# Two-layer GNN in split fp32: the DRAM layout of the adjacency and of x, and the loads that read them

## What is computed

```python
# layer 0
deg = jnp.sum(adj, axis=-1, keepdims=True)
agg = jnp.einsum('bij,bjf->bif', adj, x) / jnp.maximum(deg, EPS)
cat = jnp.concatenate([x, agg], axis=2)
out = relu(jnp.einsum('bnf,of->bno', cat, W))
x = _layernorm(x + out)
# layer 1
Ah = adj + eye
dh = rsqrt(jnp.sum(Ah, axis=-1))
An = dh[:, :, None] * Ah * dh[:, None, :]
out = relu(jnp.einsum('bnm,bmf,fc->bnc', An, x, kernel) + bias)
x = _layernorm(x + out)
```

## Time and profile of the kernel before

| | us |
|---|---|
| median of 3 runs | 506.6 |
| lowest, highest run | 506.44, 506.66 |
| profiled execution, its own time | 506.57 |
| its span in the profile | 504.8 |

### The profile page before, as it was taken

How to read it: one execution, slowest core, us unless ns; L and a number is a source line. 1 busy time by engine, 2 the same in 40 slices (tenths; PEclk the granted TensorE clock), 3 DMA queues, 4 the chain that set the end, 5 groups by cost and what they waited for, 6 DMA issues and landing times.

```text
span 504.8 us, 8135 instructions
## 1 busy us (share of the span) xinstructions
PE 491.4 (97%) x2750; PEld 430.7 (85%) x2750; DVE 393.8 (78%) x960; ACT 327.8 (65%) x601; POOL 0.7 (0%) x6
## 2 busy tenths in 40 slices
PE   7999999999999999999999999999999999999992
PEld 5988788988889888998889988898888988889992
DVE  4786898669966799667996679966898669976656
ACT  5795948757677657766586574955847757576422
POOL 0000000000000000000000000000000000000000
PEclk9999999999999999999999999999999999999997
DMA  7999517944097621955239361593607932061002
GB/s 259 409 373 359 208 48 251 374 120 174 6 349 270 201 90 66 369 188 208 83 117 396 113 211 77 200 385 82 246 1 258 366 115 93 0 208 43 1 0 83
DMA packets 26686, 93.38 MB, mean 185 GB/s; under 512 B 2864, under 2 KB 2992, under 8 KB 26672
## 3 DMA queue, kind: packets, MB, share of 16 engines
q1 hardware_dynamic: 26672, 93.20, 51.1%
HBM read 84.80 MB, written 8.39 MB: 185 GB/s over the span
## 4 chain that ended last, share of the span: by engine, by line
PE 96%; DVE 1%; DMA 1%; ACT 0%; issue 0%; ACTq 0%; SPq 0%
PE ring_b L688 23%; PE ring_b L690 23%; PE ring_b L689 23%; PE ring_a L688 9%; PE ring_a L690 9%; PE ring_a L689 9%; DMA adj_raw<-adjT 1%; DVE stats L521 0%; DVE x L513 0%; DVE u L509 0%; PE ring_b L721 0%; PE ring_b L729 0%; PE ring_b L725 0%; ACT adj_hi L268 0%; ACT x L333 0%
## 5 line engine op out<-in xcount | busy, mean ns | idle before, releaser
L688 PE MATMUL ring_b<-adj_hi,x_hi 128*128 128x512 f32 x254 | 99.4, 391 | 0.0
L689 PE MATMUL ring_b<-adj_lo,x_hi 128*128 128x512 f32 x254 | 99.0, 390 | 0.0
L690 PE MATMUL ring_b<-adj_hi,x_lo 128*128 128x512 f32 x254 | 99.0, 390 | 0.0
L688 PE MATMUL ring_b<-adj_hi,x1s_hi 128*128 128x512 f32 (+1 forms) x256 | 98.3, 384 | 0.0
L690 PE MATMUL ring_b<-adj_hi,x1s_lo 128*128 128x512 f32 (+1 forms) x256 | 98.0, 383 | 0.0
L689 PE MATMUL ring_b<-adj_lo,x1s_hi 128*128 128x512 f32 (+1 forms) x256 | 97.9, 382 | 0.0
L268 ACT ACTIVATE gath_hi<-ring_b 128x512 fp32r<-128x512 f32 (+1 forms) x64 | 36.6, 583 | 64.8 <-PE ring_b L690 64.7
L444 DVE TENSOR_TENSOR adj_lo<-adj_raw,adj_hi 128x1024 fp32r<-128x1024 f32 (+1 forms) x68 | 76.0, 1158 | 3.4 <-ACT adj_hi L268 3.4
L283 ACT ACTIVATE adj_nat<-adj_nat 128x1024 f32<-128x1024 f32 x64 | 67.1, 1052 | 5.0 <-DMA adj_nat<-adjN 4.9
L268 ACT ACTIVATE adj_hi<-adj_raw 128x1024 fp32r<-128x1024 f32 (+1 forms) x68 | 64.9, 999 | 0.8 <-DMA adj_raw<-adjT 0.6
L444 DVE TENSOR_TENSOR gath_lo<-ring_b,gath_hi 128x512 fp32r<-128x512 f32 (+1 forms) x64 | 42.7, 678 | 22.1 <-ACT gath_hi L268 22.1
(11 more groups left out here) (87 smaller groups left out, 940.2 us busy)
## 6 DMA issues: line engine op xcount, KB each, us to landing
adj_nat<-adjN SPq DMA_DIRECT2D x64, 512.0 KB, 5.8
adj_raw<-adjT SPq DMA_DIRECT2D x60, 512.0 KB, 9.7
out<-x SPq DMA_DIRECT2D x15, 512.0 KB, 3.3
xt_raw<-xT SPq DMA_DIRECT2D x7, 1024.0 KB, 4.9
x_sb<-x SPq DMA_DIRECT2D x14, 512.0 KB, 5.1
adj_raw<-adjT SPq DMA_DIRECT2D x8, 256.0 KB, 6.4
x_sb<-x SPq DMA_DIRECT2D x4, 256.0 KB, 6.2
xt_raw<-xT SPq DMA_DIRECT2D x2, 512.0 KB, 12.0
```

Source lines behind the costliest of these rows:

```text
L688: nc.tensor.matmul(o, lhi, rhi, start=(first and i == 0), stop=False)
L689: nc.tensor.matmul(o, lhi, rlo, start=False, stop=False)
L690: last = nc.tensor.matmul(o, llo, rhi, start=False, stop=last_part)
```

## The change

The host lays adjT out as (batch, half, tile, partition, 512), so that one tile of one half is 256 KB without a gap. It lays x out as (batch, pair of tiles, partition, 512), so that one pair is 256 KB without a gap. The destinations in SBUF and everything that the engines compute on stay as they are. The twelve first loads of batch 0 (lines 204 to 206) now each read one piece of 256 KB. A chunk of the adjacency (line 188) and a half of x (line 192) are now two such pieces, with 2 KB for each partition from each, where they were 4 KB for each partition.

```diff
--- before.py
+++ after.py
@@ -186,10 +186,14 @@
             def load_adj(n, h, chunks=range(CH)):
                 for i in chunks:
                     sp.dma_start(raw[:, h, i * JC:(i + 1) * JC, :],
-                                 adjT[n, h, :, i * JC:(i + 1) * JC, :]).then_inc(raw_loaded[h][i], 16)
+                                 adjT[n, h, i * JC:(i + 1) * JC].rearrange("j p m -> p j m")
+                                 ).then_inc(raw_loaded[h][i], 16)
 
             def load_x(n, h):
-                sp.dma_start(x_half(x_sb, h), x_half(x[n], h)).then_inc(x_loaded[h], 16)
+                pairs = CH // H
+                sp.dma_start(x_half(x_sb, h).rearrange("p (i t) c -> p i (t c)", i=pairs),
+                             x[n, pairs * h:pairs * (h + 1)].rearrange("i p m -> p i m")
+                             ).then_inc(x_loaded[h], 16)
 
             def load_rows(n, t):
                 i = t % NR
@@ -201,10 +205,10 @@
 
             for i in range(CH):
                 loaded = x_first_loaded[i // 2] if i % 2 == 0 else x_loaded[i // 2]
-                sp.dma_start(x_pair(x_sb, i), x_pair(x[0], i)).then_inc(loaded, 16)
-                sp.dma_start(raw[:, 0, JC * i, :], adjT[0, 0, :, JC * i, :]).then_inc(raw_first_loaded[i], 16)
+                sp.dma_start(x_pair(x_sb, i).rearrange("p t c -> p (t c)"), x[0, i]).then_inc(loaded, 16)
+                sp.dma_start(raw[:, 0, JC * i, :], adjT[0, 0, JC * i]).then_inc(raw_first_loaded[i], 16)
                 sp.dma_start(raw[:, 0, JC * i + 1, :],
-                             adjT[0, 0, :, JC * i + 1, :]).then_inc(raw_loaded[0][i], 16)
+                             adjT[0, 0, JC * i + 1]).then_inc(raw_loaded[0][i], 16)
             sp.dma_start(w_raw, w).then_inc(w_loaded, 16)
             sp.dma_start(xt_target(0, 1), xt_source(0, 0, 1)).then_inc(xt0_loaded[0], 16)
             load_rows(0, 0)
@@ -862,9 +866,9 @@
 
     x, adj, w, k, bias = (np.asarray(a) for a in (x, adj, L0_gnn_W, L1_gnn_kernel, L1_gnn_bias))
     arrays = {
-        "adjT": adj.reshape(B, H, NH, T, P).transpose(0, 1, 4, 3, 2),
+        "adjT": adj.reshape(B, H, NH, T, P).transpose(0, 1, 3, 4, 2),
         "adjN": adj.reshape(B, T, P, N).transpose(0, 2, 1, 3),
-        "x": x.reshape(B, T, P, F).transpose(0, 2, 1, 3),
+        "x": x.reshape(B, CH, JC, P, F).transpose(0, 1, 3, 2, 4).reshape(B, CH, P, JC * F),
         "xT": x.reshape(B, XP, T // XP, P, FT, P).transpose(0, 1, 5, 2, 4, 3).reshape(B, XP, P, T // XP * FT * P),
         "w": w.reshape(F, 2, FT, P).transpose(3, 2, 1, 0).reshape(P, FT, 2 * F),
         "k": k.reshape(FT, P, F).transpose(1, 0, 2),
```

## The result

The changed kernel takes 504.78 us (median of 6 runs, 504.41 to 505.13) against 506.56 us beside it, a ratio of 0.9963 with a 95% interval of 0.9952 to 0.9973. The forecast was 506.1 with 505.0 as its lower end. In a second comparison on another chip it took 504.63 us, ratio 0.9949 (0.9934 to 0.9964). The gain is 1.8 us in the first comparison and 2.3 in the second.

A forecast was written before the change was run, and what follows sets the result against it. The prediction took TensorE, busy 97% of the span, as the bound, with time to win only in the slow opening loads. It summed -0.6 us (first two loads) and +0.1 (2 KB chunks) to -0.5: 506.1 us, range 505.0 to 507.6.

The forecast's parts named there:

- The bound: Whole kernel: TensorE, busy 97% of the span; time to be had lies between the first adjacency load's issue at 1.18 and 6.23.
- the first two loads: Opening: 0.524 MB of x and adjacency without gaps; first adjacency tile lands 0.6 us sooner, range 0.1 to 0.8.
- the rate of xT's opening: Opening: xT, read without gaps, moved 213 GB/s in its first two microseconds; taken as the new loads' rate, giving 0.6 us.
- a bound from above: Opening: 0.5 MB issued at 107.00 took 4.7 us; two such loads from 0.75 would be down at 5.45, 0.8 us sooner.
- The check of what TensorE needs next: Behind TensorE's start: tile 2 has 1.5 us in hand, the projection 1.2, the fourth degree 0.7; all hold 0.6 us.
- The rival with the clock: TensorE's first products: a shorter gap brings the fast clock forward, about 1.0 on top of 0.6, 505.0 us; chance 0.22.
- The 2 KB chunks: Batch 0's four half 1 chunk loads: 5.6 us at 376 GB/s against 5.1 at 413, 0.5 us more queue.
- The row tiles of adjN: Before the fourth degree: row tile lands at 27.0, wanted at 27.2; just holds, 0.1 us charged for the thin margin.
- There is no slack there: From the fourth degree to TensorE's wait at 61.19: what ScalarE loses at 27.79 is lost to the end.
- The stop at 61.19: TensorE's 0.29 us wait for the gathered low parts, the one stop before the tail; to stay no longer than 0.4.
- The steady batches: Later batches: 1.2 us more loading each, hidden by early landings, costed at nothing; without cover up to 8 us over seven.
- the slower rival: Batch 0's queue: twelve loads without gaps each begin badly, slipping 5.3 us, or half; 508.0 us taken; chance 0.16.

The follow-up runs named there:

- first_only: Kernel before, with only batch 0's twelve first loads (x and adjacency) reading copies without gaps; 504.26 us, ratio 0.9950.
- x_only: Kernel before, with only x laid out anew and the adjacency as before; 504.99 us, ratio 0.9968.
- after_again: The changed kernel, unedited, measured once more beside the kernel before on another chip; 504.63 us, ratio 0.9949.
- x_pitch8448: Kernel before, with batch 0's four loads of x reading a copy with rows 8448 bytes apart; ratio 0.9972.
- x_pitch32k: Kernel before, with batch 0's four loads of x reading a copy with rows 32 KB apart; ratio 0.9976.
- x_pitch10k: Kernel before, with batch 0's four loads of x reading a copy with rows 10 KB apart; ratio 0.9961, one 2812 us execution left out.
- x_pitch8k: Control: kernel before, with batch 0's four loads of x reading a copy with rows still 8 KB apart; ratio 0.9994.

## Why the prediction was wrong

**The bound was read rightly.** The gain was made in the opening: first_only shows it by leaving the rest alone. The part from the first issue to TensorE's start gave 2.1 us; the speed of the first products and the supply of tiles behind them gave and took the rest before 18 us.

**The step that failed is "the first two loads".** It is one term of the sum, 0.6 us, and it measured 2.1. Two readings in it were at fault. I took the rate of xT's opening, 213 GB/s, as that of the new pattern; it was 291. The 213 holds half a microsecond at 49 GB/s, and the new opening has no such hole after its first half microsecond:

```profile
1.75:2.25 0.50, 0.50 (x5) 0.50 (x4) 0.00 (x0) 0.28 (x1) 0.00 (x0) 1.00 0.73 139
2.25:2.75 0.50, 0.50 (x4) 0.50 (x4) 0.00 (x0) 0.00 (x0) 0.00 (x0) 1.00 0.98 336
```

And I took 0.8 us as a bound from above, from x's own later load at 107.00, down after 4.7 us, whose rows are 8 KB apart too: the bound was read off the very pattern that is slow. In the changed kernel the same load, issued at 105.10, is down after 3.7 us. "Strided against without gaps" was the wrong question for x's landing; the runs put that lag on one pitch of six, 8 KB. With x on time the adjacency's 16 KB cost the start 0.2 us (5.00 in x_only, 4.80 in first_only), but its layout still gives part of the time, and no run says by which property. The opening's 146 GB/s was the hint, and the spread of the 16 landings of the first load, which the prediction didn't read, shows seven engines on time and nine not.

**The check of what TensorE needs next left out tile 1.** I named tiles 2 and on. Tile 1's low part was ready at about 8.2 before, 1.5 us ahead of its use at 9.73, and would have been wanted at 7.6 after a gain of 2.1 us. It became the one new wait, 1.10 us in this profile. With 0.6 us this would not have shown; with the true size it decides.

**The rival with the clock had the time, 505.0, and part of the mechanism.** Its sign appeared: the products were fast 1 us after the first, not 3.5. They did speed up sooner, worth 0.87 us in this profile, and in the kernel before the clock alone is worth 1.1. But the changed kernel doesn't live on it: with 8 warming matmuls, and eight slow products, it kept nearly all of its gain. It lives on the loads.

**The 2 KB chunks cost less than I charged.** I charged 0.5 us of queue by the stretch of 376 GB/s, as if the size of the pieces had held it down; with the same 2 KB and no gaps it moves 399. In the full queue 395 GB/s in place of 413 make 0.2 us for the four chunk loads. At 84 against 159 ns a transfer, twice the number costs 6% of a load's transfer time, and the engines' total share fell. The estimate from the fixed cycles per packet of the Trainium skill, "DMA: Bandwidth & Descriptors", "Why small descriptors are slow (HBM only)", was a smaller penalty of 2.3%, or 0.1 us. The trace's 4 to 6% lie between that and the 10% of my row.

**The row tiles of adjN were the next limit, as said**, with the thin margin named in the prediction. In the changed kernel's first profile the fourth degree came 1.6 us sooner than before where 1.9 were wanted, which the slack behind it covered; in after_again they cost ScalarE 0.7 us, and 0.8 us of the 2.46 were lost there. "There is no slack there" was wrong by 0.3 to 0.5 us. The stop at 61.19 moved to 59.31 and stayed 0.27 us. The steady batches hide all that they were said to hide.

**Nothing came of the slower rival.** The first load without gaps is finished by all 16 engines within 0.4 us (2.99 to 3.38).

**What stays open.** Why a pitch of 8 KB holds up part of the engines is not shown; 256 bytes of padding remove it. Nor is it shown what holds part of the engines at tile 1 of the adjacency, two by 1.4 us in the changed kernel, six by 1.1 in first_only; the number and the delay vary from profile to profile. It is open which property of the adjacency's layout gives its part of the time. And the moment at which the products speed up differed between profiles with nearly the same start (4.9 to 5.1): at once in x_pitch8448 and x_pitch32k, after two products in the changed kernel, after nine in x_pitch10k. In x_pitch8k, after 2.6 us of idling, the first five were fast and the next eight slow. I found no rule for it.

## What to carry to other kernels

Before the layout of an opening load is judged by bytes and packets, look at how evenly the 16 engines finish it: a load is as late as its last engine, and a mean rate hides that. A row pitch of 8 KB with pieces of 2 KB made a load land 1.5 to 2 us late on a cold start, and a padding of 256 bytes gave, within the intervals, what x's new layout gave by itself. When a start moves forward, check the very next operand first, then each queue that the saved time runs into; the term that grows beyond your estimate meets limits that the estimate never tested.

## What was not expected of the hardware

- Rows 8 KB apart: nine of sixteen DMA engines finish their 16 KB share 1 to 2 us late, in x before (5.00 for the last) and in a copy of x (4.89). An adjacency tile with this pitch has eight on time and its last at 6.13. Rows of x 4 KB, 8448 bytes, 10, 16 and 32 KB apart: last engine at 3.41, 3.50, 3.48, 3.72 and 3.53.
- Transfers of 2048 bytes at 84 ns and of 4096 at 159 ns have nearly the same rate, 24 and 26 GB/s for an engine; with the queue full, pieces of 2 KB moved 395 GB/s where pieces of 4 KB moved 410 to 413.
- In the kernel before, keeping TensorE busy until its first real product is worth 1.1 us of 506.6; in the changed kernel the same knob is worth nothing measurable.
